# A vision tower on one core: half of the tokens sorted by expert, the other half dense and weighted at evacuation, Mish from a sigmoid

## What is computed

```
tokenizer:  x1 = patches @ (W1_w + W1_sw * f(eps_out1) f(eps_in1)^T)^T + b1
            x2 = the same with W2 and its noise           f(e) = sign(e) sqrt|e|
            y  = (mish(x1) * x2) @ W3_w^T + W3_b, plus a positional encoding
            mish(x) = x * tanh(softplus(x))
attention:  layer norm, 8 heads with relative-position keys and values, output
            projection, added to the tokens (65 tokens an image)
MoE FFN:    layer norm, logits = x @ Wr^T + br, softmax over 8 experts, the two
            largest kept;  out = tokens + sum over the two of
            weight_e * (gelu(x @ W1_e + b1_e) @ W2_e + b2_e),   hidden width 256
```

## Time and profile before

| what | value |
|---|---|
| times of three executions | 250.34, 251.15, 251.19 us (median 251.15) |
| span of the profiled execution | 249.9 us |
| PE busy | 230.9 us (92%) |
| DVE busy | 191.3 us (77%) |
| ACT busy | 164.2 us (66%) |
| POOL busy | 62.8 us (25%) |
| DMA moved | 16.46 MB |

### The profile page before, as it was taken

One profiled execution on the slowest core, in us unless ns is written; L12 is line 12 of the kernel. 1 busy time (PEld: TensorE's weight loads), 2 busy tenths in 40 slices (PEclk: granted clock), 3 DMA queues, 4 the chain that ended last, 5 costly groups with the idle time before them and its releaser, 6 DMA issues.

```text
span 249.9 us, 6298 instructions
## 1 busy us (share of the span) xinstructions
PE 230.9 (92%) x2316; PEld 194.7 (78%) x2316; DVE 191.3 (77%) x481; ACT 164.2 (66%) x509; POOL 62.8 (25%) x94
## 2 busy tenths in 40 slices
PE   1999999999998889989989999999899999999993
PEld 1945665899776766658778899889799999999972
DVE  1576789865668899998186738678999989989991
ACT  2461469752199899993026987422799888898870
POOL 8814132096005465469112400000000000000000
PEclk9999999999999999999999999999999999999999
DMA  6980000000003326064000000069888510001011
GB/s 147 335 217 3 1 0 1 3 3 0 3 0 81 91 65 108 4 212 129 3 7 3 0 3 0 8 103 131 151 211 260 173 37 10 22 4 32 0 42 34
DMA packets 15625, 16.46 MB, mean 66 GB/s; under 512 B 1747, under 2 KB 14367, under 8 KB 15468
## 3 DMA queue, kind: packets, MB, share of 16 engines
q1 hardware_dynamic: 14424, 15.59, 26.0%
q0 software_dynamic: 544, 0.35, 0.6%
q10 hardware_dynamic: 628, 0.14, 0.3%
HBM read 13.91 MB, written 2.16 MB: 64 GB/s over the span
## 4 chain that ended last, share of the span: by engine, by line
PE 54%; DVE 13%; issue 11%; POOL 11%; DMA 4%; ACT 3%; SPq 2%; DVEq 0%; POOLq 0%
PE banks L1328 49%; POOL region_e L471 5%; DMA region_d<-in_L_tok_W_sw 4%; DVE KT L1286 2%; POOL w_lo L526 2%; DVE top L1028 1%; DVE stb L992 1%; POOL region_d L478 1%; PE banks L1531 1%; POOL rstd L413 1%; PE banks L1672 1%; DVE stb L911 1%; ACT region_d L701 1%; DVE y_lo L1269 1%; DVE stats L890 1%
## 5 line engine op out<-in xcount | busy, mean ns | idle before, releaser
L760 ACT ACTIVATE w_sb<-banks,vecs 128x416 f32<-128x416 f32 x60 | 36.4, 608 | 11.2 <-PE banks L1328 8.9
L677 ACT ACTIVATE region_e<-banks,ntop 128x64 f32<-128x64 f32 x128 | 38.3, 346 | 5.0 <-DVE ntop L1035 4.8
L768 ACT ACTIVATE y_hi<-w_sb 128x416 fp32r<-128x416 f32 x60 | 32.7, 548 | 8.1 <-DVE w_sb L1260 8.1
L1269 DVE TENSOR_TENSOR y_lo<-w_sb,y_hi 128x416 fp32r<-128x416 f32 x60 | 34.9, 585 | 1.0 <-ACT y_hi L768 1.0
L677 ACT ACTIVATION_READ_ACCUMULATOR region_e<-banks,ntop 128x1 f32 x128 | 29.8, 238 | 0.0
L1328 PE MATMUL banks<-x_hi,w_hi 128*128 128x416 f32 x80 | 29.3, 366 | 0.0
L1328 PE MATMUL banks<-x_lo,w_hi 128*128 128x416 f32 x80 | 28.1, 352 | 0.0
L1328 PE MATMUL banks<-x_hi,w_lo 128*128 128x416 f32 x80 | 28.0, 350 | 0.0
L1260 DVE TENSOR_TENSOR w_sb<-w_sb,region_c 128x416 f32<-128x416 f32 x40 | 23.4, 586 | 2.5 <-ACT w_sb L760 1.0
L1328 PE MATMUL banks<-y_hi,w_hi 128*128 128x416 f32 x60 | 22.3, 371 | 1.5 <-DVE KT L1286 1.0
L1328 PE MATMUL banks<-y_hi,w_lo 128*128 128x416 f32 x60 | 21.1, 351 | 0.0
(11 more groups left out here) (238 smaller groups left out, 502.1 us busy)
## 6 DMA issues: line engine op xcount, KB each, us to landing
region_c<-out SPq DMA_DIRECT2D x4, 832.0 KB, 14.3
xnT<-out SPq DMA_DIRECT2D x5, 208.0 KB, 13.7
QT<-out SPq DMA_DIRECT2D x5, 208.0 KB, 14.1
region_a<-in_x SPq DMA_DIRECT2D x2, 512.0 KB, 5.3
region_a<-in_x SPq DMA_DIRECT2D x1, 1024.0 KB, 9.5
out<-h SPq DMA_DIRECT2D x2, 512.0 KB, 5.8
h<-out SPq DMA_DIRECT2D x4, 256.0 KB, 5.0
w_sb<-in_L_ffn_W SPq DMA_DIRECT2D x1, 1024.0 KB, 5.6
```

The source lines that it names most:

```text
L677: last = a.activation(dst[:, h // 2, h % 2], src[:, h // 2, h % 2], ACT.Exp, scale=SCALE, bias=ntop[:, o + h:o + h + 1], accum_out=esum[:, ...
L760: a.activation(lifted(u), bank[h_bank(i)][:, 0:FB], ACT.Gelu, bias=vecs[:, b:b + 1])\
L768: a.activation(h_hi(u), lifted(u), ACT.Copy).then_inc(S["hi_ok"], 1)
L1269: v.tensor_tensor(h_lo(u), lifted(u), h_hi(u).bitcast(F32), ALU.subtract).then_inc(S["lo_ok"], 1)
```

## The change

*Mish.* With s the sigmoid of -x, mish(x) is x t'/(t' + 2) for t' = s(s-2) up to sign. ACT now computes s; DVE makes t, the denominator t + 2 and the numerator (x + b) t (`gated(n)`, three operations); POOL takes the denominator to the power -1 and multiplies (`divided(n)`, two operations of 128x512); `inner(n)` waits for that. The sign goes into `embed`.

*Half of the tokens by expert.* Token tiles 4 to 11 (1024 tokens, `SPARSE`) are not computed for all experts. DVE finds the two largest with max and max_index (`best`), PE counts ranks by a triangular matrix, DVE makes each token's two places among 23 tiles of 128 slots, sorted so that a tile has one expert (`places`, `experts`, `biases`). POOL scatters the normalised rows into DRAM (`xs_d`, cleared early by SP) with 16 indirect DMAs; SP loads them back (L473), loads each slot tile's 256 KB of weights at an offset read from a register (L440, a ring of six), PE transposes, computes up and down in plain float32, ACT does the GELU, DVE evacuates, SP stores to `ys_d`, POOL gathers with 16 indirect DMAs, and DVE weights and adds (`combined`).

*The other half, dense.* 1056 tokens pass through all 8 experts in 24 steps of FB = 352 columns with split operands. The hidden activation is no longer weighted; the result is, at evacuation. In steps before RAW = 16 DVE only evacuates (`evac`) and POOL multiplies by the weight and adds; from 16 on DVE does it (`weighed`, `summed`). The weights are broadcast over partitions through DRAM as before, now for 8 experts and 1056 tokens (L464, L467).

The order on PE is: 14 dense steps (`MID`), a bias product, the slots, the last ten dense steps. Cut to its core:

```
-            def mish(n):                                  (ACT)
-                a.activation(gate[:, b], bank[4 + n % 2][:, :], ACT.Mish, bias=nb[:, 0:1]) ...
+            def gated(n):                                 (DVE)
+                dve.wait_ge(S["sg_ok"], n + 1)
+                link(v.scalar_tensor_tensor(t, gate[:, b], 2.0, gate[:, b], op0=ALU.subtract, op1=ALU.mult))
+                v.tensor_scalar(gate[:, b], t, 2.0, None, ALU.add).then_inc(S["gt_ok"], 1)
+                v.scalar_tensor_tensor(q, bank[4 + n % 2][:, :], nb[:, 0:1], t, op0=ALU.add, op1=ALU.mult)\
+                    .then_inc(S["gate_ok"], 1)
+            def divided(n):                               (POOL)
+                pool.wait_ge(S["gt_ok"], n + 1)
+                link(g.tensor_tensor(gate[:, b], gate[:, b], mone[:, :].to_broadcast([P, BLK]), ALU.pow))
+                pool.wait_ge(S["gate_ok"], n + 1)
+                g.tensor_tensor(gate[:, b], gate[:, b], region_c[:, TOK + n * BLK:TOK + (n + 1) * BLK], ALU.mult)\
+                    .then_inc(S["gd_ok"], 1)
             def inner(n):                                 (DVE)
                 dve.wait_ge(S["in_ps"], n + 1)
+                dve.wait_ge(S["gd_ok"], n + 1)
...
+SPARSE = range(4, 12)
+SLOTS = (2 * NSP * P + E * (P - 1)) // P
+STEPS = [(blk, e) for blk in range(NB) for e in range(E)]
+RAW = 16
+MID = 14
...
+            def slot_weights(j):                          (SP)
+                if j >= W_RING:
+                    sp_.wait_ge(S["sd_ps"], j - W_RING + 1)
+                sp_.dma_start(wt[j % W_RING], w12[:, bass.ds(expert[j], 2 * FH)]).then_inc(S[f"d_up{j % W_RING}"], 16)
...
             sp_.wait_ge(S["cT_ok"], 2)
+            (four writes of combT into tw_d, and one of the class tokens)
+            sp_.wait_ge(S["d_cs"], done["d_cs"] + 16 * 5)
+            for blk in range(NB):
+                sp_.dma_start(region_c[:, 0:(E - 1) * DN]...[:, :, b], (7 experts of tw_d, 128 partitions alike))
+                sp_.dma_start(weights(E - 1)[:, b], (the eighth expert))
+            sp_.wait_ge(S["d_sc"], done["d_sc"] + 16 * 2 * NSP)
+            for i in range(3):
+                sp_.dma_start(xs[:, 8 * i * C:(8 * i + w) * C]..., xs_d[8 * i * P:(8 * i + w) * P, :]...)
+                    .then_inc(S["d_xs"], 16)
+            for g, tiles in enumerate(SG):
+                (slot weights as the ring comes free; wait for the results; store them to ys_d)
...
+            def evac(n):                                  (DVE)
+                dve.wait_ge(S["dn_ps"], n + 1)
+                v.tensor_scalar(raw(n), bank[4 + out_dense(n) % 2][:, 0:FB], vecs[:, V_FB2 + e:V_FB2 + e + 1], None, ALU.add)
+            def weighed(n):                               (DVE)
+                v.scalar_tensor_tensor(accT[:, b] if e == 0 else fresh(n), bank[...][:, 0:FB],
+                                       vecs[:, V_FB2 + e:V_FB2 + e + 1], weights(e)[:, b], op0=ALU.add, op1=ALU.mult)
+            def combined(q):                              (DVE)
+                dve.wait_ge(S[f"d_g{q}"], done[f"d_g{q}"] + 64)
+                (four scalar_tensor_tensor of 128x128: gathered rows * weight + acc)
```

More of the change, by code:

```diff
@@ L382, in _ @@
+            sp_.wait_ge(S["fin_ok"], 3)
+            for f in range(4):
+                stored(f, 2, 4)
+            for f in range(4):
+                stored(f, 12, 13)
+            sp_.wait_ge(S["fin_ok"], 4)
+            for f in range(2):
+                stored(f, 13, 16)
+            sp_.wait_ge(S["d_out"], 16 * 22)
         @block.gpsimd
@@ L433, in class_key @@
                                 kcq[:, :].unsqueeze(1).to_broadcast(bb), ALU.mult).then_inc(S["tc_ok"], 1)
-            for n in range(NBLK):
+            divided(0)
+            divided(1)
+            deviation(0)
+            divided(2)
+            divided(3)
+            for n in range(1, NBLK):
                 deviation(n)
@@ new lines, in _, with over, biased, best @@
+            iota = late[:, L_IOTA:L_IOTA + E]
+            rsum_e, rinv = rs_[:, 0:NT], rs_[:, NT:2 * NT]
+            def over(r, n):
+                return r.unsqueeze(2).to_broadcast([P, n, E])
+            def biased(lo, hi, m=P):
+                return v.tensor_tensor(lv[0:m, lo:hi, :], lp[0:m, lo:hi, :],
+                                       brb[0:m, :].unsqueeze(1).to_broadcast([m, hi - lo, E]), ALU.add)
+            def best(lo, hi):
+                for t in range(lo, hi):
+                    last = v.max(mv8[:, t, :], lv[:, t, :])
+                link(last)
+                for t in range(lo, hi):
+                    last = v.max_index(iv8[:, t, :], mv8[:, t, :], lv[:, t, :])
+                link(last)
@@ L1313, in _ @@
[L1313 to L1321 removed]
+            evac(3)
+            rest(5)
+            biases()
+            dense_route()
+            evac(4)
+            rest(6)
+            dense_route2()
+            evac(5)
@@ new lines, in _ @@
+            rest(7)
+            evac(6)
+            rest(8)
+            shares()
+            evac(7)
+            rest(9)
+            gates()
+            for n in range(8, MID - 2):
+                evac(n)
+                rest(n + 2)
+            evac(MID - 2)
+            evac(MID - 1)
+            turned(0)
+            base(0)
+            turned(1)
+            base(1)
+            for g in range(len(SG)):
+                if g + 2 < len(SG):
+                    turned(g + 2)
+                slots_out(g)
@@ new lines, in _ @@
+            rest(MID)
+            rest(MID + 1)
+            for n in range(MID, RAW):
+                evac(n)
+                rest(n + 2)
+            for n in range(RAW, len(STEPS)):
+                weighed(n)
+                if n + 2 < len(STEPS):
+                    rest(n + 2)
+                if n > RAW:
+                    summed(n)
+                if n in (RAW + 2, RAW + 3, RAW + 4, RAW + 5):
+                    combined(n - RAW - 2)
+                if n == RAW + 1:
+                    joined(0)
@@ L1697, in filled @@
+            early, later = range(0, 8), range(8, 16)
             def filled(n, part):
@@ new lines, in _ @@
+            base(0)
+            turn_slots(0)
+            base(1)
+            turn_slots(1)
+            for j in range(SLOTS + LAG):
+                if j < SLOTS:
+                    slot_up(j)
+                else:
+                    up(MID + j - SLOTS)
+                if j % 4 == 2 and j // 4 + 2 < len(SG):
+                    turn_slots(j // 4 + 2)
+                if j >= LAG:
+                    slot_down(j - LAG)
+            for n in range(MID, len(STEPS)):
+                if n + 2 < len(STEPS):
+                    up(n + 2)
+                down(n)
+                if n == RAW + 1:
+                    turn_back(0)
```

1045 lines of the change are left out of this document (628 added, 417 removed), and 4 rows, old and new, of the table AGAIN.

## The result

| kernel | median | range of runs | span profiled |
|---|---|---|---|
| before | 251.17 us | 250.34 to 254.55 | 249.9 |
| after | 601.53 us | 598.54 to 601.86 | 600.0 |

The changed kernel takes 2.390 times as long (95% interval 2.384 to 2.397). The forecast was 290 us, the range 248 to 323. The sign was right and the size was not. (One correction to the part on the change: s is the sigmoid of x itself, not of -x; with t = s(s-2), mish(x) = -x t/(t + 2).)

The account below looks back on a forecast made before the run. It took TensorE (92% busy) to bound the FFN and a serial chain across engines the front. Before's 249.9 + 17.6 (FFN and routing) + 21.9 (Mish front) = 289.4, plus 1.25 for timing, gave 290 us; range 248 to 323.

Parts of the forecast that it names:

- the price of the pow: Front, POOL's 128x512 pow in Mish: taken at 0.0073 us a column from narrow rows, 4.8 us each.
- The bound: Front: if all that four columns cost over a multiply were per column, one 128x512 pow would take 104 us.
- the prediction's signs of being wrong: Idle before the slots under 10 us, end under 25 us after last slot, or POOL's pow cheap as multiply.
- The second rival: Front: pow paid in every column; 303 us total at 8 us a pow, 323 at 13, 335 at 16; chance 0.17.
- The front's formula: Mish's four serial DVE-POOL rounds cost the front 2.7 + 4P, P one pow; `inner(3)` starts at 36.2 + 4P.
- The time without the front: Everything but the Mish front: end 17.6 us above before's 249.9, bounds from -25 to +45.
- sorted rows landed: Path to the slots: SP's loads of sorted rows, queued behind the weights' broadcasts, finish at 209.5 us.
- idle before the slots: FFN: TensorE waits some 28 us for the sorted rows before the slots' first transposes.
- from the slots to the end: Tail: ten dense steps with DVE's added work, gathers beside it or up to 10 us past it; 29 us.
- The rule of "DMA: Bandwidth & Descriptors": Broadcasts and sorted rows at 436 GB/s: some 17 us in place of 33.6, sum 274; as a rival, chance 0.07.
- The clock: TensorE's slots after the idle stretch: a fall of the granted clock taken at 0, at most 5 us.
- The first rival: FFN: TensorE never starves, so its 25 us saving comes whole; 248 us at a 4.8 us pow; chance 0.20.

Follow-up runs that it names:

- width run: Kernel before, gate as a sigmoid, with POOL pows of 1 to 56 columns and a multiply added after its last operation: 251.63 us.
- first experiment: Changed kernel with the gate back on ACT as one sigmoid operation, without DVE's and POOL's Mish operations: 269.26 us, ratio 1.065.
- the first change of order: Sorted-row loads put ahead of the six broadcasts in SP's queue, against the kernel of the first experiment: 261.89 us, ratio 1.025.
- the three after it: On top of that: a semaphore for each sorted-row load, 260.73 us; then all broadcasts issued by ACT, 260.18; or only two blocks by ACT, 263.68.

## Why the prediction was wrong

**The step that failed** is the price of the pow, in "P is not in the trace". It took the step from one column to four, 1.038 to 1.060 us, as 0.0073 us a column, and came to 4.8 us; the runs show 0.159 a column and 81.93. The one-column price came from a single row of 32x1. The trace of before has a second one-column pow, on POOL at 17.59, which I did not use:

```profile
17.59 0.58 POOL L407 TENSOR_TENSOR clsn<-clsn,mhalf 1x1 f32<-1x1 f32 x1 [6.24 <-DVE clsn L856]
```

With 0.582 for one column, the step is (1.060 - 0.582)/3 = 0.159, and P is 82: the measured value, from two rows that were there. That it comes out so near is luck in part, since the two four-column groups alone give 74 (by 1.014) and 90 (by 1.106). The 32x1 row was out of line: the same shape took 0.54 us in the width run's series and 0.55 in the changed kernel. It was no chance, though. The width run contains the program before, and there the same operation took as long again:

```profile
L534 POOL TENSOR_TENSOR rstd<-ve,mhalf 32x1 f32<-32x1 f32 x1 | 1.0, 1047 | 0.0
```

So it belongs to that place in the program; what makes it longer there is open.

**The bound was worked out and then left out.** The prediction has 104 us as P if all that four columns cost over a multiply were per column. With it the far end is 2.7 + 4 x 104 above the rest, some 690 us. The range ended at 323, because the spread of the two four-column groups (1.106 and 1.014) was read as a limit of 0.03 a column, and an error in the one-column row was not thought of. None of the prediction's signs of being wrong covers this either: they ask for a pow as cheap as a multiply, not for a dearer one. An operation scaled from 4 columns to 512 carries some 170 times (511/3) the error of its rows; the range had to hold it.

**The second rival was what happened**, pow paid in every column, with 0.17 and its price cut off at 16 us. The sentence of the Trainium skill beside it ("GPSIMD Engine Reference", section 3.1: POOL's loop goes element by element, and longer bodies are bound by their operations) points the right way, and the width run agrees in kind: 0.159 us a column for a pow beside some 0.0025 for a multiply (1.28/512; the prediction has 1.27).

**What held.** The front's formula, to 1 us in 364.81, as long as the pow is long enough to cover the loop through TensorE. The rounds that don't overlap. The time without the front: forecast 249.9 + 17.6 + 1.25 = 268.75, measured 269.26. Of its terms:

| term | forecast | first experiment |
|---|---|---|
| weights written from | 172 | 170.7 |
| sorted rows landed | 209.5 | 198.1 |
| idle before the slots | 28 | 19.1 |
| slots | 29 | 30.3 (198.1 to 228.4) |
| from the slots to the end | 29 | 37.7 (228.4 to 266.1) |

That the total is right is luck: two misses cancel. The transfers ran at 5.84 MB in 24.8 us (173.3 to 198.1), 235 GB/s where I took 174. The prediction says that no window of before shows more than 213; a narrower one does:

```profile
185.00:190.00 5.00, 5.00 (x28) 4.94 (x28) 4.64 (x10) 4.14 (x10) 0.00 (x0) 1.00 0.90 251
```

The rule of "DMA: Bandwidth & Descriptors" in the Trainium skill, some 17 us by my estimate, is too fast by 8 us here; its section states it for DMAs that GpSimd issues, and these were issued by SP. And the gathers were 1.3 us apart on the mean (the first issue at 231.7, the last at 251.6), with 3 us from the last issue to its landing; I had taken them as hidden beside DVE's work, and in the first experiment DVE waits for them twice, 2.4 and 2.3 us. Half of the gathers were worth 3.3 to 4.6 us, so of the 8.7 that the end came later, a part is left that no run separates.

The clock, at which I took 0 to 5 us, did fall: 0.65 in the window of the wait in the first experiment (174 to 203 us). The slots' part ran at 1.00 again from 203 us on.

**The first rival**, TensorE never starving, fails even without the Mish half. The wait in front of the slots was taken away in two steps, and most of it came back behind the sixth slot, at ACT, or behind the third block, as long as the bytes were the same.

## What to carry to other kernels

An operation that the trace shows only in a few columns has no price yet at 512. Ask what the result is if all of the small row is per column, and put that into the range. Two narrow widths help only where their rows agree with others of the same shape, and even then they do not decide. In before, DVE's reciprocal takes 0.203 us at 8 columns and 0.245 at 16 (L1009), its addition 0.156 and 0.200 (L1004). Extended to 512 columns both come to some 2.9 us, an estimate; measured are 3.35 for the reciprocal and 0.69 for an addition. So a product of four such operations on a serial path deserves a run of the operation by itself, near the width in question, before anything is built on it. And where several transfers stand in one queue ahead of the work, count their bytes and their issues: here the first change of order took 7 to 9 us off, the three after it only moved the wait, and fewer bytes took off most of what was left.

## What the runs showed of the hardware

- pow on POOL costs 0.39 us and 0.159 us a column, with 32 partitions or 128, with the exponent -0.5 from a tile or -1 from a repeated column; at 512 columns 65 times the multiply (81.93 and 1.26 us).
- DVE's reciprocal of 128x512 takes 3.35 us, five times an addition of that size (0.69), though at 128x16 the two are 0.245 and 0.200.
- An indirect DMA of 128 rows of 512 bytes holds POOL 0.94 to 0.97 us in most cases, and the next starts 0.3 us later: 1.25 to 1.27 us each, 1.3 on the mean of sixteen, for scatters and gathers alike.
- Behind others of its queue a DMA's issue holds its engine: the sixth broadcast's issue took 5.45 us on ACT and 5.1 on SP, beside 0.4 for the first; with 32 of its 352 columns it still took 4.39 on SP. That the queue is full then is likely, but not shown.
- In windows with long idle stretches TensorE's granted clock was 0.50 to 0.80, and the same eight matmuls took 2.05 us behind one in place of 1.09.
